# A three-part audio tower on one core: the first gated unit prepared in the last two attention batches, its scores and maxima set into the attention's tail, and the order of the first batch's small transfers changed

## Chip, cores and metric

One Trainium2 chip, one core. The metric is the device time of one execution in microseconds. TensorE (PE) multiplies, VectorE (DVE) reduces and combines, ScalarE (ACT) evaluates functions and copies, GpSimd (POOL) does elementwise work, and SyncE (SP) issues nearly all DMAs.

## The reference, cut to what matters

x is 8 batches x 750 positions x 128 channels, float32.

```python
def _proj(x, w, b, n_head):                     # q, k and v: one each
    y = jax.nn.elu(_conv1d_valid(x, w) + b)     # 3 taps: 748 positions are left
    return y.reshape(B, L, n_head, D // n_head).transpose(0, 2, 1, 3)
scores = einsum('bhqd,bhkd->bhqk', q, k) / sqrt(16)        # 8 heads of 16
h = einsum('bhqk,bhkd->bhqd', softmax(scores), v)          # then heads side by side
...
nx = layer_norm(_layernorm(h))                  # the gated unit: normalised twice
q, k, linear, pre_gelu = split(nx @ expand)     # q and k of width 16
gated = linear * gelu(pre_gelu); local, v = gated[:, :128], gated[:, 128:]
logits = q @ k.T / sqrt(16) + where(causal, sigmoid(rel + mult), -inf)
h = h + norm(h) + concat([local, softmax(logits) @ v], -1) @ project
...
h = h + moe(norm(h))                            # router, top 2 of 64, capacity 128, FFN of 512
```

## The kernel before, in words

The program has two blocks, and all engines meet between them. **The first block** is the attention of the 8 batches. A batch is 24 steps (`STEPS`). In step s PE makes one piece of scores (3 groups of matmuls into PSUM banks 0 to 2 of `ps_a`, lines 651 to 664), DVE takes row maxima from them (`row_max`, lines 537 and 539), and 9 steps later (`LAG`) PE makes the same scores turned (`scores_T`, line 648), with two extra contraction rows that subtract the maxima. ACT takes the exponentials (line 448), and `apply` (line 679) multiplies with the values, three steps in a group of 24 row instructions. Every quarter batch the maxima are turned by PE (line 722), copied by ACT to `max_T` (line 386), and brought into `q_rep` by one DMA (`maxima_rows`, line 218). The first turned scores of a quarter wait for that DMA. Beside this, `chunk` sets the next batch's q, k and v convolutions (lines 689 and 712) between the scores of the same loop, in bank `ps_misc`, and its q and k are split into bfloat16 parts and replicated by 24 DMAs (lines 155 and 159) in SP's queue, which is in program order. `spread` (line 1932) brings a half batch of outputs into `hall` by 16 DMAs.

After batch 7 only the lagging turned scores are left: the **tail**, `last_step` and `last`, where exponentials run on pairs of banks (`pair_slot`, line 445). The tail also holds the preparation of the gated unit of batch 0 ("unit 0"): PE turns its normalised input (`turn_first`, line 1038) and makes q and k (`qk_first`, line 1052), DVE and POOL split them into parts (`split_first`, `middle_first`, `rest_first`, lines 1060 to 1072). Every one of these uses the one bank `ps_misc`, so each waits until the one ahead has been read. DVE normalises at line 1028, POOL multiplies and adds at lines 1019 and 1077.

**The second block** is a pipeline over units: iteration `it` handles attention and projection of unit `it`, the router and FFN of unit `it - 1`, and q and k of unit `it + 1`. Iteration 0 has only unit 0: its scores (lines 1752 and 1755), maxima (line 1525), the turned maxima and their DMA, local and value halves (lines 1729 and 1738), turned scores (1771), exponentials (1376), `weigh` (1590), `attend` (1786), `turn_att` (1708), `project` (1799 and 1802) and the sum `sum_2` (1618), which ends it. `order_of` and `places` give each item its PSUM banks.

## Time and profile before

| | |
|---|---|
| time, median of 3 runs | 816.52 us (814.9 to 816.86) |
| the profiled execution's own time | 817.78 us |
| span of the profiled execution | 816.0 us |
| busy: PE, DVE, ACT, POOL | 779.3, 681.1, 504.8, 272.1 us |
| mean granted TensorE clock | 0.992 |

The span runs from the first to the last instruction, and about 1.8 us of the execution's time lie outside it. PE's busy time is modelled: a matmul that waits for its operand after its issue can count as busy, so that 779.3 is an upper estimate of its work.

### The profile page before, as it was taken

What the parts mean: (1) busy time and instruction counts of PE and PEld (TensorE: products, weight loads), DVE (VectorE), ACT (ScalarE), POOL (GpSimd) and SP (SyncE); (2) the same over time, 40 slices, a digit from 0 to 9 for tenths busy, and PEclk for the clock granted to TensorE, in tenths of its full rate; (3) what the DMA queues carried; (4) which work ended last, traced back from release to release, by engine and by line L of the source; (5) the groups of instructions that cost most, each with busy time, mean ns of one, the idle gap of its engine ahead of it and who ended that gap; (6) DMA issues with size and microseconds to landing.
All of it is one profiled execution on the core that took longest, in us unless ns stands there. A gap on an engine that the chain in (4) does not pass through costs nothing. (4 is left out here: it accounts for less than half of the span.)

```text
span 816.0 us, 15612 instructions
## 1 busy us (share of the span) xinstructions
PE 779.3 (95%) x5555; PEld 476.3 (58%) x5555; DVE 681.1 (83%) x1622; ACT 504.8 (62%) x1098; POOL 272.1 (33%) x281
## 2 busy tenths in 40 slices
PE   9797999999999999999999998878999999999997
PEld 5343564564564564564563343347878788787885
DVE  4895998999999999999989889557788887787856
ACT  4174776776776776776776676544644646556343
POOL 4454241241341341341342122312355252333222
PEclk9999999999999999999999999999999999999999
DMA  5327033143134144134134201100000000000001
GB/s 120 68 39 98 10 61 84 15 61 83 15 60 84 15 60 83 16 60 84 15 61 65 64 5 12 11 10 2 1 21 2 20 1 20 20 2 20 20 2 38
DMA packets 85676, 31.08 MB, mean 38 GB/s; under 512 B 58496, under 2 KB 84320, under 8 KB 85600
## 3 DMA queue, kind: packets, MB, share of 16 engines
q1 hardware_dynamic: 85024, 29.61, 20.6%
q10 hardware_dynamic: 576, 0.49, 0.4%
q8 instruction: 44, 0.72, 0.4%
q14 instruction: 32, 0.26, 0.1%
HBM read 4.76 MB, written 3.06 MB: 10 GB/s over the span
## 5 line engine op out<-in xcount | busy, mean ns | idle before, releaser
L448 ACT ACTIVATE probs<-ps_a 128x384 f32<-128x384 f32 (+1 forms) x732 | 299.9, 479 | 134.3 <-PE ps_a L648 131.9
L537 DVE TENSOR_REDUCE neg_max<-ps_a 128x1 f32<-128x512 f32 (+1 forms) x384 | 248.3, 679 | 44.7 <-PE ps_a L664 41.2
L648 PE MATMUL ps_a<-q_rep,k_rep 98*128 98x384 bf16 (+3 forms) x768 | 232.1, 326 | 7.5 <-DMA q_rep<-max_T 4.9
L664 PE MATMUL ps_a<-k_rep,q_rep 96*128 96x512 bf16 (+3 forms) x768 | 217.1, 326 | 10.4 <-DVE neg_max L537 5.4
L648 PEld LDWEIGHTS ps_a<-q_rep,k_rep 98*128 98x128 bf16 (+1 forms) x768 | 78.1, 102 | 101.0 <-issue 43.9
L679 PE MATMUL ps_pv<-probs,v_hat 128*32 128x364 f32 (+3 forms) x1536 | 136.2, 487 | 0.1
L664 PEld LDWEIGHTS ps_a<-k_rep,q_rep 96*128 96x128 bf16 (+1 forms) x768 | 74.8, 103 | 86.7 <-DVE neg_max L537 25.9
L539 DVE TENSOR_REDUCE neg_max<-ps_a 128x2 f32<-128x472 f32 x192 | 123.3, 642 | 0.0
L679 PEld LDWEIGHTS ps_pv<-probs,v_hat 128*32 128x32 f32 (+1 forms) x1536 | 43.7, 110 | 61.6 <-issue 41.8
L1941 POOL TENSOR_TENSOR out_n<-out_r,inv_sum 128x192 f32<-128x192 f32 x32 | 16.3, 511 | 183.3 <-DVE inv_sum L518 175.8
L1850 PE MATMUL banks<-w_sb,hid 128*128 128x128 f32 x384 | 46.9, 276 | 0.0
L1850 PEld LDWEIGHTS banks<-w_sb,hid 128*128 128x128 f32 x384 | 45.1, 192 | 2.3
L274 POOL TENSOR_SCALAR qk_e<-qk_e 128x748 f32<-128x748 f32 x14 | 38.0, 2714 | 24.5 <-ACT qk_e L360 24.5
L1361 ACT ACTIVATE hid<-banks,b_col 128x748 f32<-128x748 f32 x31 | 27.3, 882 | 28.1 <-PE banks L1825 28.1
L1825 PE MATMUL banks<-nx3T,w_sb 128*128 128x374 f32 x128 | 42.8, 483 | 0.0
L1786 PEld LDWEIGHTS banks<-vals,p_T 128*128 128x128 f32 x336 | 38.4, 191 | 4.3 <-DVE y_b L1483 3.6
L1786 PE MATMUL banks<-vals,p_T 128*128 128x129 f32 x336 | 39.8, 277 | 0.4 <-DVE p_T L1590 0.2
L712 PE MATMUL ps_misc<-w_v,xT 128*128 128x128 f32 (+1 forms) x252 | 34.8, 274 | 0.0
L1590 DVE TENSOR_TENSOR p_T<-p_raw,bias_fac 128x748 f32<-128x748 f32 (+5 forms) x48 | 25.5, 600 | 11.0 <-ACT p_raw L1376 11.0
L689 PE MATMUL ps_misc<-xT,w_k 128*128 128x374 f32 x84 | 33.7, 486 | 0.0
L712 PEld LDWEIGHTS ps_misc<-w_v,xT 128*128 128x128 f32 (+1 forms) x252 | 33.1, 188 | 0.5 <-DVE v_z L493 0.4
L1525 DVE TENSOR_REDUCE nmax<-banks 128x1 f32<-128x128 f32 (+5 forms) x48 | 26.7, 614 | 6.6 <-PE banks L1755 6.6
(228 smaller groups left out, 1169.2 us busy)
## 6 DMA issues: line engine op xcount, KB each, us to landing
k_rep<-parts_k SPq DMA_DIRECT2D x96, 96.0 KB, 3.5
q_rep<-parts_q SPq DMA_DIRECT2D x93, 96.0 KB, 3.7
hall<-out_n SPq DMA_DIRECT2D x256, 12.0 KB, 1.8
xT<-in_x SPq DMA_DIRECT2D x8, 375.0 KB, 3.6
out_h<-y_out SPq DMA_DIRECT2D x7, 320.0 KB
q_rep<-max_T SPq DMA_DIRECT2D x32, 6.0 KB
w_sb<-in_w_T SPq DMA_DIRECT2D x2, 256.0 KB, 3.7
out_h<-y_out SPq DMA_DIRECT2D x8, 54.0 KB
```

The costliest lines, as they stand in the source:

```text
L274: pool.tensor_scalar(t, t, 1.0, -1.0, ALU.min, ALU.add).then_inc(z_negd, 1)
L448: act.activation(probs[0:rows(kt), n % RING, 0:w], ps_a[0:rows(kt), 3 + n % 3, 0:w], ACT.Exp, scale=DH ** -0.5).then_inc(p_ready, 1)
L537: dve.tensor_reduce(neg_max[0:rows(t), 0, col:col + 1], ps_a[0:rows(t), c, :], AX.X, ALU.max, negate=True).then_inc(sc_max, 1)
L539: dve.tensor_reduce(neg_max[0:rows(t), 1, col:col + QT + 1:QT], ps_a[0:rows(t), 2, 0:2 * (L - 512)].rearrange("p (a l) -> p a l", a=2), AX ...
L648: pe.matmul(out[0:rows(kt), 0:QW[qh]], k_rep[0:KM, cb % 2, h, kt * P:kt * P + rows(kt)], q_rep[0:KM, cb % 2, qh, h, 0:QW[qh]], start=True, ...
L664: last = pe.matmul(out, q_rep[0:KS, it % 2, t // QT, h, t % QT * P:t % QT * P + rows(t)], k_rep[0:KS, it % 2, h, 512:L] if c == 2 else k_r ...
L679: last = pe.matmul(ps_pv[32 * j:32 * j + 32, 0:w], v_hat[0:rows(kt), cb % 2, kt * NH + GH * g + j, :], probs[0:rows(kt), n % RING, 0:w], s ...
L689: ins = pe.matmul(bank_of(n, i)[:, 0:HALF], w_sb["qk"[i // 2]][:, tap, :], xT[:, n % 2, lo:lo + HALF], start=(tap == 0), stop=(tap == TAPS ...
L712: last = pe.matmul(bank_of(n, 4 + r)[0:rows(t), (t % 4) * P:(t % 4 + 1) * P], xT[:, n % 2, tap + t * P:tap + t * P + rows(t)], w_sb["v"][: ...
L1786: last = pe.matmul(o[:, c:c + P + 1], p_T[0:rows(k), q:q + P], vals[0:rows(k), k, :], start=(k == 0), stop=(k == t))
L1825: last = pe.matmul(o[:, 512 * h:512 * h + HALF], w1_sb[:, f * P:(f + 1) * P], nx3T[:, h * HALF:(h + 1) * HALF], start=True, stop=True)
L1850: last = pe.matmul(o[:, (t - t0) * P:(t - t0 + 1) * P], hid[:, f, (t * P):(t + 1) * P], w2_sb[:, f, :], start=(f == 0), stop=(f == NF - 1))
```

## The change

Five things are moved. In each place the work is the same unless said.

1. The six DMAs of k for heads 0 to 3, then `maxima_rows(0, 2)`, then the six for heads 4 to 7, in the first batch only; ahead of it the third convolution of batch 1 (three taps) moves from steps 0 to 2 of batch 0 into the start. The loads of the unit's weights (`load`) go from SP's start of batch 7 to its end of batch 6.
2. POOL's `constants` go from batch 7 to batch 6. Unit 0's `normalise` (DVE), `second_norm` and `residual` (POOL) go from the tail to batch 6.
3. `turn_first` and `qk_first` go from the tail to batch 7. ACT copies their results now; POOL makes all the parts with six whole-width operations for q and six for k.
4. In the tail, unit 0's scores and row maxima stand between the pairs of turned scores, in banks 0 and 1. The pairs have two slots instead of three (banks 2 to 5). The `apply` of a step stands by itself, no longer in threes, one of them ahead of the first pair. Unit 0's maxima are turned and brought to `qk_rep` there. Unit 1 is normalised there. The last `Gelu` table load of the block is gone.
5. Iteration 0 of the second block begins with unit 0's turned scores and exponentials; values and local halves come behind them. Both halves of batch 7's `spread` are issued there.

```diff
 def pair_slot(n):
-    return ps_a[:, n // 2 % 3 * 2:n // 2 % 3 * 2 + 2, :]
+    return ps_a[:, 4 - n // 2 % 2 * 2:6 - n // 2 % 2 * 2, :]
...
+                for t in range(TERMS):
+                    replicate_k(sp, n, 0, t)
+                if it == 0:
+                    maxima_rows(it, 2)
+                for t in range(TERMS):
+                    replicate_k(sp, n, 1, t)
...
+            if it == B - 1 and at in ((3, 0), (5, 0)):
+                ahead["turned_first"](act, ps_misc, s // 5)
+            if it == B - 1 and at in ((6, 1), (9, 0), (11, 0), (12, 1)):
+                ahead["z_first"](act, ps_misc, ((6, 1), (9, 0), (11, 0), (12, 1)).index(at))
...
-            if it == B and s in (1, 2):
-                ahead["turn_first"](pe, take, s - 1)
-            if it == B and s in (3, 4, 5, 6):
-                ahead["qk_first"](pe, take, s - 3)
+            if it == B - 1 and s in (1, 3):
+                ahead["turn_first"](pe, take, s // 3)
+            if it == B - 1 and s in (5, 7, 9, 10):
+                ahead["qk_first"](pe, take, (5, 7, 9, 10).index(s))
...
-        for i in range(2):
+        for i in range(3):
             for tap in range(TAPS):
                 conv_tap(1, i, tap)
...
+    def split_first(pool, j):
...
+        parts = qk_rep[0:KS, j, 0:L]
+        pool.wait_ge(first_z, 2 * j + 2)
+        step(0, pool.tensor_copy(part_a[:, j, :], left_a[:, j, :]))
+        step(1, pool.tensor_scalar(parts, part_a[:, j, :], take_out[:, j, 0:1], None, ALU.mult))
+        step(2, pool.tensor_tensor(left_a[:, j, :], left_a[:, j, :], parts, ALU.add))
+        step(3, pool.tensor_copy(part_b[:, j, :], left_a[:, j, :]))
+        step(4, pool.tensor_scalar(parts, part_b[:, j, :], take_out[:, j, 1:2], None, ALU.mult))
+        pool.tensor_tensor(parts, left_a[:, j, :], parts, ALU.add).then_inc(S["x_rep"], 1)
```

SP's queue in the first batch, behind the loads: `parts_q` and `parts_k` rows are the replications for batch 1, `max_T` rows the maxima. Before:

```order
L218 DMA q_rep<-max_T 2x12x128 x2
L155 DMA q_rep<-parts_q 16x8x384 x12
L172 DMA xT<-in_x 128x750
L159 DMA k_rep<-parts_k 16x4x768 x12
L218 DMA q_rep<-max_T 2x12x128 x2
```

and of the change:

```order
L216 DMA q_rep<-max_T 2x12x128 x2
L156 DMA q_rep<-parts_q 16x8x384 x12
L176 DMA xT<-in_x 128x750
L160 DMA k_rep<-parts_k 16x4x768 x6
L216 DMA q_rep<-max_T 2x12x128
L160 DMA k_rep<-parts_k 16x4x768 x6
L216 DMA q_rep<-max_T 2x12x128
```

The third quarter's maxima are now behind six k transfers, not twelve.

PE's queue where the tail begins: `q_rep,k_rep` rows are turned scores, `probs,v_hat` rows are `apply`, `max_parts` is the turn of batch 7's last maxima. Before:

```order
L679 MATMUL ps_pv<-probs,v_hat 32x384 x12
L722 MATMUL ps_misc<-ident_bf,max_parts 128x128
L648 MATMUL ps_a<-q_rep,k_rep 128x384 x6
L1038 MATMUL ps_misc<-ident,nx 128x128 x4
L648 MATMUL ps_a<-q_rep,k_rep 108x384 x4
L1038 MATMUL ps_misc<-ident,nx 128x128 x2
```

and of the change:

```order
L699 MATMUL ps_pv<-probs,v_hat 32x384 x4
L668 MATMUL ps_a<-q_rep,k_rep 128x384 x2
L742 MATMUL ps_misc<-ident_bf,max_parts 128x128
L668 MATMUL ps_a<-q_rep,k_rep 128x384 x2
L1125 MATMUL ps_a<-qk_rep 128x128
L1128 MATMUL ps_a<-mask_q,ident_bf 128x128
L1125 MATMUL ps_a<-qk_rep 128x256
L1128 MATMUL ps_a<-mask_q,ident_bf 128x128
```

The turn of the maxima has one `apply` and one pair ahead of it instead of a pair and three `apply`, and unit 0's scores (L1125, L1128) stand where its turned input stood.

ACT's queue across the meeting of the engines (the branches). Before:

```order
L445 ACTIVATE probs<-ps_a 108x2x364 x2
L451 ACT_TABLE_LOAD
L451 ACTIVATE warm<-ident 128x1
L1946 UNCONDITIONAL_BRANCH
L1322 UNCONDITIONAL_BRANCH
L1338 ACTIVATE gel_l<-banks 128x374 x2
L1367 COPY nmax_T<-banks 12x128
L1345 ACTIVATE gel<-banks 128x512
```

and of the change:

```order
L461 ACTIVATE probs<-ps_a 108x2x364 x2
L2014 UNCONDITIONAL_BRANCH
L1406 UNCONDITIONAL_BRANCH
L1451 ACTIVATE p_raw<-banks 128x748
L1451 ACTIVATE p_raw<-banks 128x620
L1451 ACTIVATE p_raw<-banks 128x492
L1451 ACTIVATE p_raw<-banks 128x364
```

The exponentials of unit 0 come first, without a table load ahead of them; the load for `Gelu` and the gated halves are behind them.

## Rows read from the trace of the kernel before

**Rows 1.** Timeline of PE, first batch; start, us, and in brackets the idle time ahead.

```profile
18.54 2.05 PE L689 MATMUL ps_a<-xT,w_q 128*128 128x374 f32 x6
23.50 0.79 PE L664 MATMUL ps_a<-k_rep,q_rep 96*128 96x512 bf16 x4 [2.92 <-DMA q_rep<-parts_q]
...
76.31 0.60 PE L648 MATMUL ps_a<-q_rep,k_rep 98*128 98x384 bf16 x2 [4.63 <-DMA q_rep<-max_T]
...
77.98 3.00 PE L679 MATMUL ps_pv<-probs,v_hat 128*32 128x364 f32 x24
```

**Rows 2.** Windows in which PE's granted clock was low (PEclk is the share of 2.4 GHz).

```profile
76.00:78.00 2.00, 1.69 (x10) 0.70 (x10) 0.63 (x1) 1.18 (x3) 0.00 (x0) 0.64 0.03 8
...
533.00:536.00 3.00, 2.46 (x14) 1.61 (x15) 2.44 (x13) 0.00 (x0) 0.22 (x1) 0.66 0.00 0
```

**Rows 3.** Timeline of DVE in steps 0 to 3 of batch 0.

```profile
28.12 1.29 DVE L537 TENSOR_REDUCE neg_max<-ps_a 128x1 f32<-128x512 f32 x2 [0.61 <-PE ps_a L664]
...
30.42 1.29 DVE L537 TENSOR_REDUCE neg_max<-ps_a 128x1 f32<-128x512 f32 x2 [0.45 <-PE ps_a L664]
```

**Rows 4.** Timeline of SP's queue, batch 0 and the end of batch 6.

```profile
63.00 7.60 SPq L159 DMA_DIRECT2D k_rep<-parts_k  x12
70.64 19.97 SPq L218 DMA_DIRECT2D q_rep<-max_T  x2
...
442.20 10.45 SPq L1932 DMA_DIRECT2D hall<-out_n  x16
456.15 0.66 SPq L218 DMA_DIRECT2D q_rep<-max_T  x1
```

**Rows 5.** Timeline of ACT, in batch 0 and in iteration 0 of the second block.

```profile
67.44 0.26 ACT L386 COPY max_T<-ps_misc 24x128 bf16<-24x128 bf16 x1
...
545.45 1.28 ACT L1425 ACT_TABLE_LOAD   x1
```

**Rows 6.** Timeline of PE, turns of the maxima in batches 6 and 7.

```profile
395.80 0.22 PE L722 MATMUL ps_misc<-ident_bf,max_parts 128*128 128x128 bf16 x1
411.55 0.22 PE L722 MATMUL ps_misc<-ident_bf,max_parts 128*128 128x128 bf16 x1
...
455.61 0.22 PE L722 MATMUL ps_misc<-ident_bf,max_parts 128*128 128x128 bf16 x1
469.47 0.22 PE L722 MATMUL ps_misc<-ident_bf,max_parts 128*128 128x128 bf16 x1
```

**Rows 7.** Timeline of POOL in batch 6.

```profile
407.71 1.61 POOL L279 TENSOR_TENSOR qk_e<-qk_z,parts_q 128x748 f32<-128x748 f32 x1
```

**Rows 8.** Timeline of DVE in batch 6, at the tail's start and at iteration 0's end.

```profile
408.69 0.66 DVE L525 TENSOR_TENSOR neg_both<-neg_max 128x12 f32<-128x12 f32 x1
...
509.45 1.62 DVE L1028 TENSOR_SCALAR nx<-hall,rs_all 128x128 f32<-128x128 f32 x6
...
560.28 0.96 DVE L1618 TENSOR_TENSOR h<-banks,hn 128x768 f32<-128x768 f32 x1 [1.90 <-PE banks L1802]
```

**Rows 9.** Timeline of PE, tail and iteration 0 of the second block.

```profile
508.65 0.50 PE L648 MATMUL ps_a<-q_rep,k_rep 98*128 98x384 bf16 x2 [1.72 <-DVE neg_max L539]
509.08 3.18 PE L679 MATMUL ps_pv<-probs,v_hat 128*32 128x384 f32 x24
...
516.57 2.15 PE L679 MATMUL ps_pv<-probs,v_hat 128*32 128x384 f32 x24
...
521.10 0.87 PE L1052 MATMUL ps_misc<-nx2T,qk_w 128*96 128x374 f32 x2 [0.72 <-DVE left_a L1062]
...
533.54 0.22 PE L1752 MATMUL banks<-qk_rep 96*128 96x128 bf16 x1 [2.06 <-DVE hid L1453]
...
543.75 0.84 PE L1708 MATMUL banks<-ident,nx 128*128 128x128 f32 x6 [1.62 <-POOL nx L1019]
...
547.73 1.47 PE L1721 MATMUL banks<-nx2T,qk_w 128*96 128x374 f32 x4 [1.79 <-issue]
...
556.72 0.85 PE L1708 MATMUL banks<-ident,att 128*128 128x128 f32 x6 [1.44 <-DVE att L1609]
```

More of the change, by code:

```diff
@@ L30 @@
 RING = 16
+TURNED_0 = (6, 1)
 CONVS = 6
@@ L223, in _ @@
                 maxima_rows(it - 1, 3)
-            if it == B - 1:
-                ahead["load"](sp)
             if it > 0:
@@ L313, in _ @@
             if it == B - 1:
-                ahead["constants"](pool)
+                ahead["split_first"](pool, 1)
             weigh_outputs(pool, it, 0)
+            if it == B - 2:
+                ahead["second_norm"](pool, 0, plain_wait)
+                ahead["residual"](pool, 0)
             if it > 1:
@@ L318, in _ @@
             weigh_outputs(pool, it, 1)
-        ahead["second_norm"](pool, 0, plain_wait)
-        ahead["residual"](pool, 0)
-        for i in range(4):
-            ahead["middle_first"](pool, i)
+        ahead["second_norm"](pool, 1, plain_wait)
+        ahead["residual"](pool, 1)
         weigh_outputs(pool, B - 1, 2)
@@ L804, in three_steps, with first_scores @@
             chunk(it, s + 2)
+        def first_scores(t):
+            if t == 0:
+                pe.wait_ge(sc_max, B * 72)
+            elif t > 1:
+                pe.wait_ge(ahead["S"]["y_max"], t - 1 if t < 4 else t)
+            ahead["scores"](pe, first_bank(t), 0, t)
         def last_step(s, c):
+            if s == 0:
+                apply(B - 1, 12)
             if c:
@@ L814, in last_step @@
                 scores_T(B, *c, 3)
-            chunk(B, s)
+            if s == 5:
+                apply(B - 1, 18)
+            if s in (0, 1):
+                first_scores(2 * s)
+                first_scores(2 * s + 1)
+            if s in (2, 3):
+                first_scores(s + 2)
+            if s == 5:
+                ahead["turn_max"](pe, take(ahead["S"]["y_maxT"], 1), 0)
         for it in range(B):
@@ L819, in _ @@
                 three_steps(it, s)
-        for s in range(STEPS):
+        for s in range(11):
             last_step(s, probs_step(B, s))
@@ new lines, in scores @@
+    def scores(pe, o, n, t):
+        if t == 0:
+            pe.wait_ge(S["x_rep"], n * 2 + 2)
+        w = min(P * (t + 1), L)
+        for a, b in [(0, w)] if w <= 512 else [(0, 512), (512, w)]:
+            diag = b == w
+            last = pe.matmul(o[0:rows(t), a:b], qk_rep[0:KS, 0, t * P:t * P + rows(t)], qk_rep[0:KS, 1, a:b],
+                             start=True, stop=not diag)
+            if diag:
+                last = pe.matmul(o[0:rows(t), t * P:w], ident_bf[0:rows(t), 0:rows(t)], mask_q[0:rows(t), 0:rows(t)],
+                                 start=False, stop=True)
+        last.then_inc(S["y_sc"], 1)
@@ L1395, in turned_att @@
             act.copy(attT[:, :], flat("turn_att", n)[:, 0:LP]).then_inc(S["y_attT"], 1)
-        for it in range(-1, B + 1):
-            x, y, z = 0 < it + 1 < B, 0 <= it < B, 0 <= it - 1 < B
-            if it == 0:
-                local(it, 0)
-                local(it, 1)
-                turned_max(it)
-                values(it, 0)
-                values(it, 1)
-            elif y:
+        for k in range(NT):
+            exponential(0, k)
+        act.wait_ge(loaded, 16 * 7)
+        act.wait_ge(setup, N_SETUP)
+        act.activation(table[:, 1:2], table[:, 0:1], ACT.Gelu)
+        for j in range(2):
+            values(0, j)
+        for j in range(2):
+            local(0, j)
+        turned_2(1)
+        for j in range(2):
+            high(1, j)
+        turned_att(0)
+        for j in range(2):
+            middle(1, j)
+        for it in range(1, B + 1):
+            x, y, z = 0 < it + 1 < B, 0 <= it < B, 0 <= it - 1 < B
+            if y:
                 local(it, 0)
@@ L1626, in _ @@
             if it == 0:
-                for t in range(NT):
-                    row_max(it, t)
-                maxima(it)
-                local(it, 0)
-                local(it, 1)
-                G["normalise"](dve, 1)
-                values(it, 0)
-                values(it, 1)
-            elif y:
+                for k in range(NT):
+                    weigh(it, k)
+                for j in range(2):
+                    values(it, j)
+                for j in range(2):
+                    local(it, j)
+                G["normalise"](dve, it + 2)
+                attended(it)
+                for j in range(2):
+                    left(it + 1, j)
+                for j in range(2):
+                    rest(it + 1, j)
+                sum_2(it)
+                continue
+            if y:
                 local(it, 0)
@@ L1647, in _ @@
                 transform(it - 2, 2)
-            if y and it > 0:
+            if y:
                 for t in range(3, NT):
-                    row_max(it, t)
-                maxima(it)
+                    G["row_max"](dve, flat("scores", it, t), it, t)
+                G["maxima"](dve, it)
             if z:
```

249 lines of the change are left out of this document (126 added, 123 removed).

## The prediction

> **What bounds the kernel now.** I read the timeline of PE first, because its slices are nearly full throughout, and looked in it for the places where it stands still. In the loop over batches PE and DVE take turns, and stalls are short. Four places are different, and the change touches all of them.
>
> The start of batch 0: PE is ready when its convolutions end at 20.6 us and waits 2.92 us for a transfer [rows 1], then has to do a convolution of batch 1 between the first scores, for which DVE waits 0.61 and 0.45 us [rows 3]. Late in batch 0, PE waits 4.63 us for the rows of maxima [rows 1]. ACT had copied them by 67.70 [rows 5], but SP was issuing twelve k transfers from 63.00 to 70.60 and the maxima came behind them [rows 4]; PE went on at 76.31, 5.7 us after their issue. Behind that stall PE runs at the lower of its two clocks: the granted share of 2.4 GHz is 0.64 from 76 to 78 us, where nothing but the stall's end and what follows it is matmul [rows 2], and three `apply` take 3.00 us there [rows 1] where 2.15 is usual [rows 9].
>
> The tail: PE waits 1.72 us for DVE's last maxima, then does three `apply` in 3.18 us where the same group later takes 2.15 [rows 9], which is again the lower clock. Then unit 0's transposes and products stand in its queue, each of which needs bank `ps_misc` read by DVE first; 0.72 us is the longest of four short waits there. It ends at 531.48 and starts again at 533.54 [rows 9].
>
> Iteration 0 of the second block: one unit alone, so its chain is open. PE waits 1.62 us for POOL, 1.79 us after the maxima's transfer and ACT's table load, and 1.44 us for DVE [rows 9]; the table load stands on ACT from 545.45 to 546.73 with PE and DVE behind it [rows 5]. It ends with the sum at 561.24 [rows 8].
>
> **The first batch.** (a) The three taps of the moved convolution take 2.05 us, as the same three do at 18.54 [rows 1]. They can start once DVE has read `ps_misc`, which the order in its queue puts right behind PE's last convolution, and they end by about 22.7, inside the 2.92 us wait. That cover is complete. DVE was waiting for exactly this work in steps 1 and 2, so 0.61 + 0.45 = **1.1 us** come back (between 0.5 and 1.1).
>
> (b) With six k transfers ahead the rows can be issued at 67.70, when ACT is ready, not at 70.64. They also find less in the queue. Six transfers fewer at their issue pace of 7.60 / 12 = 0.63 us are 3.8 us; the queue was running behind the issue (5.7 us to PE's restart), so they may be worth up to 0.75 each, 4.5 us. Least is the earlier issue alone, 2.9. I take 4.2 of 4.63. The low clock goes with the stall: 3.00 - 2.15 = 0.85 us in the `apply` group, and about as much in the 1.67 us of matmuls from 76.31 to 77.98 ahead of it [rows 1], 1.6 us together; 0 if the clock falls anyway, 1.8 at most. Together **5.8 us** (2.9 to 6.4). The six k transfers behind the rows are needed only in the next batch.
>
> **Batches 6 and 7.** What does added PE work cost there? Between turns of the maxima batch 6 takes 411.55 - 395.80 = 15.75 us with six taps in the way, batch 7 takes 469.47 - 455.61 = 13.86 without [rows 6]. Six taps at 2.05 / 3 are 4.1 us, and 1.9 of it shows: 46%. (c) Unit 0's PE work is four products at about 0.7 (0.87 less the overlap with the next [rows 9]) and 0.6 for transposes, 3.4 us; at 46% it costs **1.6 us** (0 to 3.4), with ACT's six copies beside the exponentials. (d) `normalise` in batch 6 is 1.62 us of DVE [rows 8], by the same share **0.8 us** (0 to 1.6). `constants`, `second_norm` and `residual` lie on POOL, which is idle most of the time there: nothing.
>
> (e) The load of the weights stands ahead of batch 6's last maxima in SP's queue. SP is free of the last `spread` at 452.65; seven issues at 0.5 to 0.63 us bring it to 456.2 to 457.1, and the maxima were issued at 456.15 before [rows 4]. So the issue is at most 0.9 us late, but about 1 MB is in flight ahead of them. The bounds are nothing and the 4.63 us of twelve k transfers (1.15 MB, with more ahead of them). The load comes in larger pieces, so I take **1.0 us**.
>
> (f) POOL gets twelve operations on 96 x 748. An operation on 128 x 748 takes 1.61 us [rows 7], so some 20 us, from step 9 of batch 7 (about 475 us) to 495, long ahead of 508 when they are needed. What it does to DVE: the first of the three small maxima operations takes 0.66 us at 408.69 and ends at 409.35, when POOL's operation from 407.71 ends at 409.32 [rows 7, 8]. Two groups of maxima fall into those 20 us. Some part of an operation each, **0.7 us** (0 to 6.4, four whole operations). The Trainium skill, SBUF — State Buffer, Who interferes with whom, says that a VectorE instruction with two SBUF inputs and a GpSimd instruction that reads SBUF exclude each other for the whole instruction, and that a reduction does not take part. By that rule the trace agrees; it speaks against moving these operations from DVE to POOL beside a busy DVE, but the row maxima, most of DVE's work, would be spared.
>
> **The tail.** (g) PE had 531.48 - 508.65 = 22.8 us behind its first wait. Now one `apply` (0.72, a third of 2.15) and one pair (0.4) lie ahead of the turn, which waits for DVE's split maxima, done by 509.45 at the latest [rows 8]. From there: 22.8 - 1.1 for these two, - 3.4 for unit 0's old work, - 2.0 for the four waits on `ps_misc`, - 1.4 for the low clock (1.03 of it in one `apply` group), + 1.6 for unit 0's scores (2,668 and 768 columns at 2.4 GHz are 1.43 us, and switches), + 1.0 for new waits, of the pairs on two slots and of `apply` 18 on a DVE that has `normalise` ahead of it. That is 17.5, so PE ends at 527.0, **4.5 us** earlier (2.5 to 5.5). I count on the clock to stay up because PE idles about 1 us here and not 1.72. Unit 0's maxima and their transfer are hidden: three steps of exponentials follow. ACT is not last: in the tail of before it waits for PE between its exponentials, and PE's 17.5 us hold less other work now.
>
> **Iteration 0.** (h) From PE's end to its next start it is 2.06 us [rows 9]: the last outputs on DVE, the meeting and DVE's memsets. The turned scores don't wait for the memsets: 0.75 saved. The scores of unit 0 and their masks are gone from PE: 1.43 us of columns at full clock, but the granted share is 0.66 there [rows 2], so 2.5 with it. Values and local halves behind them began at the low clock too, 1.0. The three waits of 1.62, 1.79 and 1.44 go: unit 1 is normalised already, the maxima are in place, and the table load lies under PE's values. That is 4.8. Against it, DVE has unit 1's parts ahead of the sum and comes 1.0 later than PE. **8.0 us** (6 to 9). From here the order of iteration 1 is as before and starts from the same sum, so the shift stays. Both `spread` are done about 21 us after the meeting, before anything asks for them.
>
> **Sum.** 1.1 + 5.8 + 4.5 + 8.0 = 19.4 gained; 1.6 + 0.8 + 1.0 + 0.7 = 4.1 given back; net 15.3. The profiled execution took 817.8, so 802.5; it lies 1.3 above the median of the runs, so **801.2 us**.
>
> **Rivals.** 1. The first batch keeps its stall. For it: rows issued at 67.70 still have six k, twelve q and an x transfer ahead, in a queue that was late by several us. Against: k transfers were half of what followed. Then 4 or more come back: 806. Chance 0.10.
>
> 2. The tail doesn't shorten. With two slots each pair of turned scores waits for the exponential of two pairs ago; if `apply`, pair and exponential run one behind the other rather than side by side and each of 9 steps takes 0.5 us more, (g) is gone: 806. Three slots were not waited for, so the trace can't tell. Chance 0.09.
>
> 3. DVE is held by POOL at each of four operations for their full length: 807. This is the rule of the skill's SBUF page at its worst. The row at 408.69 shows half an operation. Chance 0.05.
>
> 4. The gain of iteration 0 is given back in iterations 1 and 2, because something there didn't hang on the sum (statistics of batch 7 on the later `spread`, POOL's order): 809. Against: PE waits for the sum's statistics there in both. Chance 0.04. That the change doesn't do what it says would be this and 2 together, 813.
>
> 5. Slower. In batch 7 the six items share `ps_misc` with the turned maxima, and their reader is now ACT, behind its exponentials in program order, while PE stands in order. If each of the six holds PE by more than (19.4 - 2.5) / 6 = 2.8 us the kernel is slower; at 4 us, and the clock falling behind each, 823. Against: the longest such wait in the tail was 0.72, and the reader's place in ACT's queue is never more than one exponential behind. Chance 0.03.
>
> **Numbers.** The forecast has 0.69. Its own range is 797 to 805; the one given reaches to rivals 1 to 3, 796.5 to 807. What a measurement can tell from no change is about 0.3% (2.4 us). All cases but 5 lie below 814: faster 0.96, same 0.01, slower 0.03.
>
> **What would show it.** Right: PE's wait on `max_T` in batch 0 under 1 us and no window of low clock behind it; DVE without waits in steps 1 and 2; unit 0's scores between pairs and PE's last `apply` near 524 us (531.5 less the terms up to there); `p_raw` right behind the meeting and no PE wait over 1 us up to `project`. From PE's last `apply` to the end of the sum about 22 us instead of 29.8. Wrong: waits of PE on ACT's copies in batch 7, a wait on `max_T` of 2 us or more at its step 3, small DVE operations of 1 us and more beside POOL, or a low clock in the tail.

## The result, and the profile after

The changed kernel takes 804.4 us (median of 4 runs, 804.01 to 804.79), the kernel before 816.7 (4 runs, 814.9 to 816.89). The ratio is 0.9853, with a 95% interval of 0.9833 to 0.9873: 12.3 us less. The profiled execution took 804.39 us, its span is 802.7 us; against 817.78 for the profiled execution before, that is 13.4 us. The forecast was 801.2 (15.3 us less, both in the profile's own time and against the median).

I followed the difference with one ruler: the times at which PE turns the maxima (the successors of [rows 6]), of both traces. Each difference between two neighbours is a stretch of the program.

| stretch | before | after | gained | predicted |
|---|---|---|---|---|
| start, to the end of the shared convolutions | 20.59 | 21.83 | -1.24 | 0 |
| from there to the turn at step 7 of batch 0 | 16.68 | 17.61 | -0.93 | (a) +1.1 |
| step 19 of batch 0 to step 1 of batch 1 | 22.25 | 17.21 | +5.04 | (b) +5.8 |
| batch 6, step 13 to 19 | 13.38 | 14.92 | -1.54 | (d) -0.8 |
| batch 6 step 19 to batch 7 step 1 | 14.63 | 14.88 | -0.25 | |
| batch 7, step 1 to 7 | 13.86 | 13.96 | -0.10 | (e) -1.0 |
| batch 7, step 7 to 13 | 14.10 | 14.62 | -0.52 | (c), (f) -2.3 |
| batch 7 step 19 to PE's last `apply` | 34.53 | 30.27 | +4.26 | (g) +4.5 |
| last `apply` to the end of iteration 0's sum | 29.76 | 21.25 | +8.51 | (h) +8.0 |

Everything else keeps its distances within 0.02 us; behind the sum the shift stays at 13.3 to 13.4 to the end of the span. (Distances are worked out from unrounded times, so the last digit can differ by 0.01 from a difference of rows.)

The first row is lost before any step that differs, in the first k convolution (PE's timeline of the changed kernel, then of the kernel before):

```profile
5.32 4.96 PE L720 MATMUL ps_a<-xT,w_k 128*128 128x384 f32 x12
...
5.10 3.94 PE L700 MATMUL ps_a<-xT,w_k 128*128 128x384 f32 x12
```

One by one, its first matmuls start 0.64 us apart up to the one at 7.24, and 0.32 apart from 7.63 on; in the kernel before all are 0.32 apart. That is the ratio of the two clock levels, and the trace's record of the granted clock begins in the changed kernel with its rise to 2.4 GHz at 7.38 us, in the kernel before at 4.87. A rise 2.51 us later at half the speed is the 1.24 us. (The windows print 1.00 ahead of the rise, where nothing is on record.)

PE's timeline in the first batch (start, us, and in brackets the idle time ahead), where [rows 1] stood:

```profile
19.78 2.05 PE L709 MATMUL ps_a<-xT,w_q 128*128 128x374 f32 x6
21.88 2.15 PE L709 MATMUL ps_misc<-xT,w_k 128*128 128x374 f32 x6
25.04 0.79 PE L684 MATMUL ps_a<-k_rep,q_rep 96*128 96x512 bf16 x4 [1.01 <-DMA q_rep<-parts_q]
...
75.06 0.48 PE L668 MATMUL ps_a<-q_rep,k_rep 98*128 98x384 bf16 x2 [0.99 <-DMA q_rep<-max_T]
...
76.06 2.04 PE L699 MATMUL ps_pv<-probs,v_hat 128*32 128x364 f32 x24
```

The moved convolution stands in the wait, of which 1.01 us is left. The wait of 4.63 us is 0.99, and the three `apply` behind it take 2.04 us at full clock. But the windows of the start show something that was not there before (columns as in [rows 2]):

```profile
24.00:28.00 4.00, 2.03 (x10) 0.68 (x9) 2.55 (x5) 0.57 (x1) 3.66 (x2) 0.98 0.21 51
28.00:32.00 4.00, 3.96 (x9) 0.74 (x9) 4.00 (x8) 0.00 (x0) 0.00 (x0) 0.50 0.59 130
32.00:36.00 4.00, 4.00 (x11) 1.93 (x11) 3.39 (x6) 0.00 (x0) 0.00 (x0) 0.50 0.98 118
36.00:40.00 4.00, 3.48 (x11) 1.44 (x9) 2.81 (x8) 1.65 (x3) 0.25 (x1) 0.74 0.01 2
```

PE runs at 1.2 GHz from 27.9 to 38.1 us, for 10.2 us. In the kernel before the same level lasted from 25.3 to 28.7. Behind it DVE waits, which it no longer did in steps 1 and 2 [rows 3]:

```profile
34.91 1.29 DVE L552 TENSOR_REDUCE neg_max<-ps_a 128x1 f32<-128x512 f32 x2 [0.61 <-PE ps_a L684]
...
38.47 1.29 DVE L552 TENSOR_REDUCE neg_max<-ps_a 128x1 f32<-128x512 f32 x2 [1.09 <-PE ps_a L684]
```

SP's queue (against [rows 4]): the rows go out at 69.89, as soon as ACT has them, between two halves of the k transfers, and later the load stands ahead of batch 6's last rows.

```profile
65.16 3.76 SPq L160 DMA_DIRECT2D k_rep<-parts_k  x6
69.89 0.65 SPq L216 DMA_DIRECT2D q_rep<-max_T  x1
...
454.37 0.43 SPq L947 DMA_DIRECT2D b_row<-in_b  x1
455.04 0.67 SPq L216 DMA_DIRECT2D q_rep<-max_T  x1
```

DVE in batches 6 and 7: the three pairs of `normalise`, the wait of `repeat_weights` for the load, and a small maxima operation beside POOL. A pair undisturbed takes 0.59.

```profile
424.05 0.89 DVE L1072 TENSOR_SCALAR nx<-hall,rs_all 128x128 f32<-128x128 f32 x2
...
426.62 1.31 DVE L1072 TENSOR_SCALAR nx<-hall,rs_all 128x128 f32<-128x128 f32 x2
...
429.61 0.59 DVE L1072 TENSOR_SCALAR nx<-hall,rs_all 128x128 f32<-128x128 f32 x2
...
459.19 0.33 DVE L1023 COPY qk_w<-expand_sb 128x96 f32<-128x96 f32 x2 [0.46 <-DMA b_row<-in_b]
...
480.44 0.54 DVE L542 CAST max_parts<-neg_both 128x12 bf16<-128x12 f32 x1
```

Beside the first two pairs POOL is at work:

```profile
424.00 1.92 POOL L279 TENSOR_SCALAR v_e<-v_e 128x512 f32<-128x512 f32 x1 [1.98 <-ACT v_e L377]
425.88 1.61 POOL L289 TENSOR_TENSOR parts_k<-qk_e,parts_k 128x748 bf16<-128x748 f32 x1
```

PE in batch 6, in the tail and at iteration 0's start (against [rows 9]). The first row is what the pair at 426.62 did: DVE came to its row maxima late and PE stood 1.13 us.

```profile
428.59 0.39 PE L684 MATMUL ps_a<-k_rep,q_rep 96*128 96x512 bf16 x1 [1.13 <-DVE neg_max L552]
...
506.87 0.85 PE L699 MATMUL ps_pv<-probs,v_hat 128*32 128x384 f32 x8 [0.44 <-ACT probs L464]
...
508.94 0.22 PE L742 MATMUL ps_misc<-ident_bf,max_parts 128*128 128x128 bf16 x1 [0.78 <-DVE max_parts L544]
...
519.22 0.82 PE L699 MATMUL ps_pv<-probs,v_hat 128*32 128x364 f32 x8 [0.55 <-DVE out_r L531]
...
525.90 0.82 PE L699 MATMUL ps_pv<-probs,v_hat 108*32 108x364 f32 x8 [0.18 <-ACT probs L461]
528.22 0.38 PE L1835 MATMUL banks<-qk_rep 98*128 98x512 bf16 x1 [1.50 <-PEq L2014]
```

The wait of 1.72 us has become two, 0.44 and 0.78, with an `apply` and a pair between them; the granted clock stays at 1.00 from 506 us through iteration 0. After 528.22 PE has no wait up to `project`, and DVE's sum ends at 547.97:

```profile
547.02 0.95 DVE L1689 TENSOR_TENSOR h<-banks,hn 128x768 f32<-128x768 f32 x1
```

### The profile page after: what moved, and what is told of

Read it like the earlier page. It is cut to its first block and busy times, and to the rows that moved or that the text cites. A ratio compares the mean times of both kernels' runs of the same rounds, so it can differ in the third digit from the quotient of the medians.

```text
span 802.7 us, 15609 instructions
## 1 busy us (share of the span) xinstructions
PE 778.9 (97%) x5555; PEld 475.5 (59%) x5555; DVE 674.7 (84%) x1608; ACT 504.3 (63%) x1100; POOL 288.6 (36%) x291
## 3 DMA queue, kind: packets, MB, share of 16 engines
HBM read 4.76 MB, written 3.06 MB: 10 GB/s over the span
## 5 line engine op out<-in xcount | busy, mean ns | idle before, releaser
L1889 PEld LDWEIGHTS banks<-nx3T,w_sb 128*128 128x128 f32 x128 | 23.1, 190 | 13.8 <-issue 1.5
```

Source lines behind the costliest of these rows:

```text
L1889: last = pe.matmul(o[:, 512 * h:512 * h + HALF], w1_sb[:, f * P:(f + 1) * P], nx3T[:, h * HALF:(h + 1) * HALF], start=True, stop=True)
```

## The experiments

Each is an edit of the changed kernel, with the median and the ratio to the kernel before on the same chip. The changed kernel's own ratio is 0.9853, so a ratio of 0.9890 is 3 us more; the sets of runs were taken on different chips. "Less" and "more" are differences of medians; the ratios can give up to 0.8 us more or less than they do (experiment 4: 4.4 us by the ratio, 3.6 by the medians), and what is under 1.5 us lies inside the intervals and rests on the traces. Beside the time I read the distances of the turns, which repeat within 0.03 us where nothing was edited, but for three: the stretch up to step 7 of batch 0, the one from step 19 of batch 0 on (17.03 to 17.27 us where not edited), and steps 1 to 6 of batch 7 (13.95 to 14.62).

**1. The convolution back, term (a).**

```diff
-                if it == 0 and at in ((1, 0), (5, 3)):
+                if it == 0 and at in ((3, 0), (5, 3)):
                     first_copy_k(s // 5)
...
-                    if it > 0 or s > 2:
-                        conv_tap(n, 2 + s // 3, s % 3)
+                    conv_tap(n, 2 + s // 3, s % 3)
...
-        for i in range(3):
+        for i in range(2):
             for tap in range(TAPS):
                 conv_tap(1, i, tap)
```

> The changed kernel with the third convolution of batch 1 back in steps 0 to 2 of batch 0 (all else as changed). In the changed kernel's trace DVE lost its waits of steps 1 and 2, as predicted, but the granted clock is 0.50 from 28 to 38 us (before: 2.9 us at the low level) and DVE waits 0.61 and 1.09 us behind it; and everything is 1.24 us late from the first convolutions on. Theory A: the low stretch of 10 us comes with the moved convolution and costs about 0.9 us net; the 1.24 us of the start does not hang on it: about 803.5 us, against 804.4. Theory B: the late start comes with it too: about 802.3. Rival, term (a) of the prediction: the moved convolution gains 1.1, so without it 805.5.

804.19 us (803.01 to 804.86), ratio 0.9860 (0.9841 to 0.9878): by time no difference. By the trace the turn at step 7 comes at 37.98, 1.46 us earlier than in the changed kernel, and 0.86 of it is there before the edited place. The other 0.60 can't all be put down to the edit, because the clock rose earlier in this profile (5.64 against 7.38): at an equal rise it is 0.2, as (a) below works out. The low stretch is 26.1 to 29.5 us, 3.4 us, as in the kernel before (the 2.9 in the expectation is a misreading). The prediction's +1.1 is out; theory A has the sign, and its 0.9 was too much.

**2. The rows behind all k transfers, term (b).**

```diff
-                if it == 0:
-                    maxima_rows(it, 2)
                 for t in range(TERMS):
                     replicate_k(sp, n, 1, t)
-            if it > 0:
-                maxima_rows(it, 2)
+            maxima_rows(it, 2)
```

> The changed kernel with the rows of maxima of batch 0's second quarter issued behind all twelve k transfers again. Theory (term (b) of the prediction, 5.8 us, of which the turns of the two traces show 5.05): the wait on max_T is 4 to 5 us again, a stretch of low clock behind it, about 809.8 us against 804.4. Rival: only the earlier issue counts (2.9 us) and the clock stays up: about 807.3.

811.48 us (809.39 to 812.26), ratio 0.9945 (0.9928 to 0.9961): 7.1 us more. The stretch from step 19 to step 1 of batch 1 is 23.99 us against 17.21, 6.78 more. PE's timeline, and below it the windows (us, PE busy, its clock, DMA share, GB/s):

```profile
77.26 0.80 PE L665 MATMUL ps_a<-q_rep,k_rep 98*128 98x384 bf16 x2 [4.99 <-DMA q_rep<-max_T]
...
79.12 3.87 PE L696 MATMUL ps_pv<-probs,v_hat 128*32 128x364 f32 x24
```

```profile
76.00:78.00 2.00, 0.74 (x3) 0.52 0.01 1
78.00:80.00 2.00, 2.00 (x13) 0.50 0.03 8
80.00:82.00 2.00, 2.00 (x16) 0.50 0.00 0
82.00:84.00 2.00, 2.00 (x15) 0.77 0.00 0
```

The wait accounts for 4.0 us, the clock for most of the rest: the whole `apply` group ran at 1.2 GHz, 3.87 us in place of 2.04, where before only part of it did, 3.00 [rows 1]. Undone, this one edit costs 7 of the 12.3 us; as made, it gave 5.04 (the table), because the low stretch behind the stall lasts 6.8 us here and lasted 3.4 in the kernel before. In this profile the clock also falls at the meeting before the second block, 1.6 us that don't hang on the edit; and the turn at step 7 of batch 0 is 1.9 us earlier, where the clock rose at 4.41 us in place of 7.38.

**3. Normalise where PE is the slower, term (d).**

```diff
-            if it == B - 2 and at in ((13, 0), (14, 0), (15, 0)):
-                ahead["normalise"](dve, 0, 2 * (s - 13), 2 * (s - 13) + 2)
+            if it == B - 2 and at in ((8, 1), (9, 2), (10, 1)):
+                ahead["normalise"](dve, 0, 2 * (s - 8), 2 * (s - 8) + 2)
```

> The changed kernel with unit 0's normalise on DVE at steps 8, 9 and 10 of batch 6 in place of steps 13, 14 and 15. Theory: in steps 13 to 15 the three pairs took 0.89, 1.31 and 0.59 us (two of them beside a POOL operation) and DVE is what PE waits for there: 1.54 us later than before at the next turn. In steps 8 to 10 DVE waits for PE 0.76 and 0.69 us and POOL is idle beside the chosen places, so nearly all of it comes back: about 802.9 us against 804.4, pairs of 0.6 us each. Rival: DVE and PE share the bound everywhere in batch 6, so DVE's 1.6 us cost the same 0.8 as predicted wherever they stand: 803.7; or what was lost is not normalise but second_norm and residual on POOL: no change, 804.4.

803.26 us (802.86 to 804.74), ratio 0.9844 (0.9829 to 0.9860), 1.1 us less; the intervals overlap. The pairs take 0.59 each. Steps 7 to 12 take 16.48 in place of 16.05, steps 13 to 18 are back at 13.38 from 14.92: 1.11 gained. Then steps 1 to 6 of batch 7 take 14.61 in place of 13.96, so over half of it is gone again in the profile: DVE still waits 0.45 for the load and PE 0.50 for the rows behind it. It is PE's wait that counts: the first turned scores that need the rows start 3.80 us behind the turn in place of 3.14, which is the whole 0.66. What was gained upstream ran into a transfer that had not become earlier.

**4. The load back in batch 7, term (e).**

```diff
         for it in range(B):
             n = it + 1
             if it > 0:
                 maxima_rows(it - 1, 3)
+            if it == B - 1:
+                ahead["load"](sp)
...
-            if it == B - 2:
-                ahead["load"](sp)
```

> The changed kernel with the load of the second block's weights back in batch 7, behind batch 6's last maxima on SP. Term (e) of the prediction says it gives back 1.0 us (803.4). What I read in the changed kernel's trace speaks against it: maxima issued at 455.04, 14.9 us behind the ones before, as in the kernel before (14.6), and PE does not wait for their transfer: no difference, 804.4 within 0.5, turns of batch 7 at the same distances.

808.02 us (806.73 to 809.93), ratio 0.9907 (0.9889 to 0.9924): 3.6 us more. Both expectations are out. DVE's timeline shows what neither had:

```profile
462.51 0.33 DVE L1023 COPY qk_w<-expand_sb 128x96 f32<-128x96 f32 x2 [3.65 <-DMA b_row<-in_b]
```

`repeat_weights` was moved from the tail into batch 7, and it waits for all seven loads. With the load late, DVE stands 3.65 us, and the turns are 17.44 us apart in place of 13.96. I had looked for this term's price on PE's wait for the rows; with the load late it is on DVE.

**5. Without unit 0's products and parts, terms (c) and (f).** `qk_first` and `z_first` are taken out of batch 7, and each `split_first` becomes a memset:

```diff
-            if it == B - 1 and s in (5, 7, 9, 10):
-                ahead["qk_first"](pe, take, (5, 7, 9, 10).index(s))
...
-        step(0, pool.tensor_copy(part_a[:, j, :], left_a[:, j, :]))
...
+        pool.memset(parts, 1.0).then_inc(S["x_rep"], 1)
```

> The changed kernel without unit 0's four products, their four copies on ACT and the twelve POOL operations behind them in batch 7 (one memset of qk_rep stands in their place, so unit 0's scores are not those of the reference; the two transposes stay). It prices terms (c) and (f). By the prediction four products at 0.7 us and 46% are 1.3 us and POOL's operations 0.7, together 2.0: 802.4 us against 804.4. By the turns of the changed kernel's trace only steps 7 to 12 of batch 7 became longer, 14.62 against 14.10 us: about 803.9, and this distance goes back to 14.10.

803.71 us (802.67 to 804.49), ratio 0.9842 (0.9819 to 0.9864). Steps 7 to 12 take 13.87 in place of 14.62, but steps 1 to 6 14.46 in place of 13.96, so 0.23 net in the profile and 0.7 by the medians. The half microsecond at steps 1 to 6 is PE's wait for the maxima rows behind the load again:

```profile
456.69 0.47 PE L666 MATMUL ps_a<-q_rep,k_rep 98*128 98x364 bf16 x2 [0.36 <-ACT probs L462]
```

The view names ACT. But these turned scores start 3.65 us behind the turn in place of 3.14, and the semaphore of the rows has its last update 3.52 behind the turn. In all five traces with such a delay (experiments 3, 5, 6, 7 and 8) PE starts 0.13 to 0.14 us behind that update, which comes at 3.06 to 3.67; in the changed kernel it comes at 2.77, ahead of PE's need. So these 0.5 us are not a price of (c) or (f), and the two together cost the 0.75 of steps 7 to 12 (0.7 by the medians, 0.9 by the ratios), not 2.3. Why the rows land at different times behind the same issue is open.

**6. Without POOL's parts, term (f).** The six operations of each `split_first` become one copy.

> The changed kernel with one copy in place of the six POOL operations of each half of unit 0's parts (ten of the twelve are left out, unit 0's q and k are not split into parts), everything else as changed. It prices (f) alone. Theory: one small maxima operation of DVE in batch 7 took 0.54 in place of 0.17 us beside a POOL operation and nothing else was held, so 0.4 us: 804.0, the distance of the turns at steps 7 and 13 goes from 14.62 to 14.25. Rival 1: the prediction's 0.7 or more: 803.7 or less. Rival 2: DVE's 0.37 us lie beside PE's products, and the distance stays 14.62: 804.4.

804.71 us (803.68 to 806.10), ratio 0.9853 (0.9829 to 0.9876). The cast is back at 0.17 us and the distance stays at 14.62, so rival 2 holds: (f) costs nothing. What makes these steps longer are unit 0's products or their copies.

**7. The turn ahead of the first `apply`, the order in the tail (g).**

```diff
             if s == 0:
+                turn(B, s)
                 apply(B - 1, 12)
```

> The changed kernel with the tail's first items on PE in the order of the kernel before: the last turn of the maxima ahead of apply 12 and of the first pair of turned scores. Theory: PE then stands 1.2 to 2 us in one piece at about 507 us, as the kernel before did (1.72), the granted clock falls behind it (before: 1.03 us lost in one group of three apply), and the time is 1.5 to 2 us longer, about 806. Rival A: the clock stays up and only the idle time shows: 805.0. Rival B: the tail is paced by ACT's exponentials and the transfer of the maxima is in time anyway: 804.4.

806.86 us (806.24 to 809.38), ratio 0.9883 (0.9861 to 0.9905), 2.5 us more. PE's timeline and windows:

```profile
508.78 0.22 PE L742 MATMUL ps_misc<-ident_bf,max_parts 128*128 128x128 bf16 x1 [2.51 <-DVE max_parts L544]
```

```profile
508.00:510.00 2.00, 1.22 (x11) 1.00 0.16 21
510.00:512.00 2.00, 2.00 (x14) 0.56 0.00 0
512.00:514.00 2.00, 2.00 (x12) 0.59 0.01 3
514.00:516.00 2.00, 2.00 (x17) 1.00 0.00 0
```

From the last turn of the loop (step 19 of batch 7) to the last `apply` it is 33.03 us against 30.27. Of the tail's 4.26 us, 2.76 hang on these two items standing ahead of the wait: 1.29 of it is idle time (2.51 against 0.44 + 0.78). The rest, 1.47, I put down to the clock, which is low for 3.4 us there. What gave the other 1.5 us of the tail no run has undone.

**8. The small Gelu activation back, term (h).**

```diff
                     after_exp(it, s, j)
+        act.activation(warm[:, :], ident[:, 0:1], ACT.Gelu)
```

> The changed kernel with the small Gelu activation at the end of ACT's tail put back. It prices the table loads in term (h). ACT is idle for 2.94 us between its last exponential and iteration 0's first, and one load takes 1.28. Theory: the load of Gelu lies in that idle time, the load of the exponential's table comes on top when iteration 0 starts, and p_raw, on which DVE waits 1.18 us, comes 1.3 us later: 805.6 against 804.4. Rival A: both loads fit into the idle time: 804.4. Rival B: neither does: 807.0.

804.98 us (803.96 to 805.30), ratio 0.9853 (0.9833 to 0.9873). ACT's timeline:

```profile
523.88 1.28 ACT L467 ACT_TABLE_LOAD   x1
...
525.93 1.28 ACT L1452 ACT_TABLE_LOAD   x1 [0.56 <-PEq L2015]
527.23 2.61 ACT L1452 ACTIVATE p_raw<-banks 128x748 f32<-128x748 f32 x6
```

`p_raw` comes 1.00 us behind PE's first scores in place of 0.57; 0.81 is what experiments 11 and 12 show, where the clock falls within 0.2 us of those scores as it does here. From the last `apply` to the end of the sum it is 22.80 us, no more than in the other five traces in which the clock falls behind the meeting (22.81 to 22.94). So both loads fit, rival A, and the table loads are no part of the gain once the order has changed. By the timelines (h) is made of 4.85 us of waits that are gone, 0.56 at the meeting, and 3.1 of PE's work and clock; no run has undone its order.

**9. Four edits together.** Edits 1 and 3, and:

```diff
-                for t in range(TERMS):
-                    replicate_k(sp, n, 0, t)
                 if it == 0:
                     maxima_rows(it, 2)
-                for t in range(TERMS):
-                    replicate_k(sp, n, 1, t)
+                for g in range(NG):
+                    for t in range(TERMS):
+                        replicate_k(sp, n, g, t)
...
+            if it == B - 2:
+                ahead["load"](sp)
             if it > 0:
                 spread(sp, it - 1, 1)
-            if it == B - 2:
-                ahead["load"](sp)
```

> Four edits on the changed kernel together: the third convolution of batch 1 back in batch 0; unit 0's normalise at steps 8 to 10 of batch 6; the weights' load ahead of batch 6's spread instead of behind it; the rows of batch 0's second quarter ahead of all k transfers. Theory: 0.3 for the first, 1.1 for the second and 0.5 more because batch 7 no longer waits for the load and the rows behind it, 0.5 for DVE's wait on the load, 0.9 for PE's wait on max_T in batch 0: 3.0 to 3.3 us together, about 801.2 against 804.4. Rival: the k transfers of batch 1, 5 us later, are late for its first scores, and the waits of batch 7 were covered: about 803.

801.48 us (801.29 to 802.11), ratio 0.9816 (0.9795 to 0.9838): 3 us less than the changed kernel. The wait on `max_T` in batch 0 is gone (15.83 us against 17.21 between the turns) and k is not late. But the rows of batch 6's last quarter go out behind the spread, at 452.50 with the turn at 450.24, PE waits 0.99 us for them, and the distance there is 15.11. So the theory's total came out, but not its parts: by the turns 1.38 come from batch 0 and 1.11 from batch 6, batch 7 loses 1.15 where 0.5 was to be gained, and the turn at step 7 of batch 0 is 1.81 earlier, of which about 1.6 go with the clock's earlier rise (5.15 against 7.38 us). The right total is in part luck.

**10 to 12. The changed kernel again, and the load in SP's own gap, without and with the moved convolution.** These ran on one chip. Experiments 11 and 12 have the edits of experiment 9 but for the load, which stands here (12 leaves out edit 1):

```diff
             maxima_rows(it, 0)
+            if it == B - 2:
+                ahead["load"](sp)
```

> The changed kernel once more, without an edit, on the chip of the three that follow: what their times are held against, and how far the start and the first low stretch of the clock differ between two profiles of one program. By the profiles so far the first convolution ends 0.1 to 1.3 us later than in the kernel before whatever the edit, and the low stretch of the three kernels with the moved convolution was 7.5 to 10.7 us: I expect 804.4 within 0.6, a low stretch of 7 to 11 us, and the turns from batch 0's second on at the same distances as before within 0.1.

804.39 us (804.01 to 805.93), ratio 0.9851 (0.9832 to 0.9869), and the distances repeat within 0.03. The low stretch is 10.2 us. (Those of the earlier profiles with the moved convolution are 6.8 or 10.2 us by the trace's record, not 7.5 to 10.7 as the expectation has it.) The first convolutions are as late as in the first profile, within 0.04, and the clock rises at 7.30 us, in the first profile at 7.38.

> As the kernel with all four edits, but with the weights' load behind batch 6's first maxima rows, where SP is idle for 4.2 us, in place of ahead of its spread, where it made the spread and the rows behind it 2 us late (PE waited 0.99 us for max_T, and the turns at steps 1 and 7 of batch 7 were 15.11 us apart). Theory: this distance becomes 13.9 to 14.1, the wait on max_T is gone, and the kernel takes 1.0 us less than with all four edits, about 3.9 less than the changed kernel: 800.4. Rival: rows are late because the spread's transfers fill the queues, not because of SP's order: the distance stays over 14.6, 801.4.

802.60 us (801.98 to 803.26), ratio 0.9824 (0.9806 to 0.9842). The wait is gone and the distance is 13.96, as the theory has it, so the turn at step 19 of batch 7 is 0.86 us earlier than in experiment 9. Yet the time is not 800.4. The windows at iteration 0's start show why, for the profiled execution:

```profile
522.00:524.00 2.00, 0.76 (x8) 1.00 0.00 0
524.00:526.00 2.00, 1.74 (x9) 0.60 0.08 9
526.00:528.00 2.00, 2.00 (x11) 0.54 0.24 28
528.00:530.00 2.00, 2.00 (x12) 1.00 0.10 9
```

PE stands 1.50 us at the meeting, as in every kernel here, and this time the clock falls: 20.36 us from PE's first matmul to the start of the sum, against 18.80 in experiment 9 and in the changed kernel.

> As the kernel before it in this set, but with the third convolution of batch 1 in the start, as in the changed kernel. It is the second comparison of this edit alone. Theory: the granted clock is 0.50 for 7 to 11 us from about 28 us in place of some 3 us, DVE waits for PE behind it, and 0.6 us are lost: 801.0. Rival: the two are even (medians of the first comparison: 804.19 without, 804.40 with it), 800.4. The prediction's rival: it gains 1.1, 799.3.

803.18 us (802.29 to 803.53), ratio 0.9828 (0.9811 to 0.9846), 0.6 us more than the one before it, with a low stretch of 10.2 us. That is theory A's difference, but the intervals overlap, and the traces have 0.39 us at the turn of step 7 with the start taken off, of which about half goes with the clock's later rise (6.47 against 5.58 us).

## Why the prediction was right or wrong

The sign and the four places are right, and 12.3 us came of the 15.3 forecast, all from the late wait in the first batch, the tail and iteration 0, while batches 6 and 7 give some back. The forecast was 3.2 us too low. By the table, 13.2 us came in the profile where 15.3 were forecast, 2.1 less; the other 1.1 is the profiled execution before, which lay 1.1 us above its median of 816.7 while the one after lay at it. The 2.1 are what is left of larger misses: the start, (a), (b), (d), (g) and the 0.25 between batches 6 and 7 came 5.3 us worse than forecast, (c) with (f), (e) and (h) 3.2 better. That part of the closeness is luck. By the steps:

**(a)** said "inside the 2.92 us wait. That cover is complete", and so it was. What failed is the step "1.1 us come back": it takes PE's speed behind the wait as given. With the convolution in the wait PE works, stands 1.01 us, works in pieces between DVE's maxima and then runs at 1.2 GHz for 10.2 us instead of 3.4, and at that level its taps at 32.98 and 35.49 make DVE wait 0.61 and 1.09. In all ten traces with the convolution in the start (the changed kernel and nine of the runs) the low stretch is 6.8 or 10.2 us, in the four without it (the kernel before and three) 3.4.

The 0.93 us of the table are not all the convolution's price. The time of the turn at step 7 also follows the time at which the clock first rises, so only profiles with an equal rise can be compared:

| convolution in the start, low stretch 10.2 us: rise | 5.05 | 5.54 | 6.09 | 6.41 | 6.47 | 7.30 | 7.38 | 7.44 |
|---|---|---|---|---|---|---|---|---|
| turn at step 7 | 37.73 | 38.09 | 38.49 | 38.73 | 38.78 | 39.40 | 39.44 | 39.49 |

Each microsecond of later rise costs 0.74 here, 0.5 of it in the first convolution. Without the convolution the turns are at 37.63, 37.95 and 37.98 for rises at 5.15, 5.58 and 5.64: 0.17 to 0.18 earlier than the table gives between its columns. So by the traces the moved convolution loses 0.2 us where 1.1 were forecast, and my estimate for the later rise is 1.9 of the 2.2 us that the changed kernel's profile has lost at this turn (2.51 x 0.74). The other two traces with the convolution, with rises at 4.19 and 4.41 and low stretches of 6.8 us, have the turn at 37.21 and 37.53; no edited kernel without it has so early a rise to hold against them. Why the low stretch is longer with the convolution is not settled.

**(b)** was right in mechanism. The wait fell by 3.64 (I took 4.2) and the clock gave 1.4 (I took 1.6). Undoing it costs 6.8 to 7.1, because how long the low level lasts behind such a stall differs: 3.4 us in the kernel before, 6.8 in experiment 2.

**(c) and (f)** were too dear: 0.7 to 0.9 for both. "At 46%" came from the convolutions' taps, and PE's work of unit 0 was covered better. (f) is nothing; POOL held one operation, for 0.37 us, and without POOL's work steps 7 to 12 took the same 14.62 us.

**(d)** was too cheap: 1.54, not 0.8. I priced 1.62 us of DVE time by PE's share, and missed that POOL works beside the first two pairs. That this is what was missed is worked out and not shown by a run alone, since experiment 3 changed place and neighbour at once: the two pairs take 1.02 us longer than undisturbed ones, and DVE's idle time in this stretch was 0.92 us before and is 0.10 now. Without POOL about 0.5 of the 1.54 would be left, by my estimate. The pair at 426.62 ends at 427.93, when POOL's operation from 425.88 has ended at 427.49. The Trainium skill, SBUF — State Buffer, Who interferes with whom, lists tensor_scalar and cast among the operations that can take the pair of ports that GpSimd needs, with one input too. The trace agrees that they can be held (0.89 and 1.31 against 0.59 us, and the cast's 0.54 against 0.17), though not each time: the second operation of the pair at 424.05 took its usual 0.33 in the middle of POOL's. I had used only the page's half on two inputs. In experiment 7's profile, whose batch 6 is unedited, PE's same stop of 1.13 us let the clock fall (0.58 from 428 to 430 us) and the stretch took 16.38 us.

**(e)** was too dear: nothing was lost. The prediction priced the rows behind the load at 1.0. In the changed kernel they land 2.77 us behind the turn and PE needs them at 3.14; in five of its variants they were 0.05 to 0.66 late, so the danger was real and the margin small. DVE's wait for the load, 0.46 us, is at an operation that the change moved into batch 7 (`repeat_weights`, which the list of the change does not name). It costs nothing: with waits of 0.18 and 0 (experiments 10 and 1), and with the load 40 us earlier (11 and 12), the turns are the same 13.96 apart. The 0.10 over the kernel before is therefore not the load's. With the load late, in experiment 4, the same wait costs 3.5. I costed the load as a step that moved and not its reader.

**(g)** and **(h)** held: 4.26 for 4.5 and 8.51 for 8.0. (The last `apply` ends at 526.7 us and not near 524, for what was missed ahead of the tail.) The last `apply` ends 30.27 us behind the last turn of batch 7, by the prediction's 527.0 it would have been 30.05. What it is worth that the turn stands behind an `apply` and a pair is shown by experiment 7 (2.76 us); the rest of (g), and (h) as a whole, are read from the timelines. In (h) the counted items came true one by one (no wait on POOL, on the maxima's transfer or on `att`), but 1.56 us of it hang on the clock, which falls behind the meeting in 6 of the 13 traces of the changed kernel and its variants.

**Start.** The prediction had nothing here, and 1.24 us were lost before any step that differs: the clock rose 2.51 us later. The same kernel shows it again (a rise at 7.30 us, experiment 10), but its variants don't all: over the 13 traces of the changed kernel and its variants the rise lies between 4.19 and 7.44 us and the q convolution's start between 8.83 and 10.15, and from 5.05 to 7.44 the start comes 0.5 us later for each microsecond of the rise. Whether the executions behind the medians had early or late rises isn't on record. Open are the 0.25 us from step 19 of batch 6 on, which are there in every variant, and the 0.10 at steps 1 to 6 of batch 7.

**Rivals.** 1 and 2 fell (the stall is gone, the tail is shorter; two slots cost no wait over 0.55). 3 and 5 fell with experiments 5 and 6 and PE's waits on ACT's copies, 0.2 us at most. 4 fell: 13.27 at the sum, 13.4 at the end.

## What to carry to other kernels

When an operation moves, price three things: its own time, what its readers wait for (here the load whose reader had moved too: nothing lost in time, 3.5 us with the load late), and what works beside it at the new place: 1.6 us of DVE work cost 1.54 beside POOL, and 0.43 five steps earlier, where POOL was idle and PE the slower. Small transfers behind a batch of large ones on one queue are the cheapest thing to look for: moving one of them gave 5.0 us here, and putting it back cost 7. And filling a wait with work doesn't end it if what follows is paced by another engine: look at the clock behind it, not only at the wait. Last, before a difference of a microsecond is put down to an edit, compare when the clock rose and fell in the two profiles.

## What the runs showed of the hardware

TensorE starts at its lower level, and when it first rises differs between profiles: 4.19 to 7.44 us from the span's start, with the same first instructions. Matmuls of one form start 0.64 us apart before it and 0.32 behind it.

Stops of the same length don't always have the same effect on TensorE's clock. A stop of 1.50 us at the meeting, with the same work on both sides, was followed by about 3.4 us at 1.2 GHz in 6 of 13 traces and by none in 7, at a price of 1.56 to 1.69 us; one of 1.13 us in batch 6 left the clock up in the changed kernel and let it fall in experiment 7. The Trainium skill, TensorE: Matmul & The Clock Gate, What's actually happening, says that the chip's look at PE's activity runs on by itself and doesn't start with the kernel, so that the point of a change varies from run to run. The traces agree in that much, by the spread of the first rise and by these stops. It makes a single profile a poor judge of 1.5 us here: experiment 11 was 0.86 us ahead of experiment 9 at the end of the loop and 0.70 us behind at the start of the sum.
